# A GRU over 128 steps on one core: dummy products between the first sums, the candidate's first input products by groups, evictions between the splits of the recurrent weights, and a last step without splits

## What is computed

```python
def step(h, inp):
    x_t, prop = inp
    comb = jnp.concatenate([x_t, h], axis=-1)
    z = jax.nn.sigmoid(comb @ Wz + bz)
    r = jax.nn.sigmoid(comb @ Wr + br)
    comb2 = jnp.concatenate([x_t, r * h], axis=-1)
    h_cand = jnp.tanh(comb2 @ Wh + bh)
    h_new = (1.0 - z) * h + z * h_cand
    h_next = jnp.where(prop, jnp.tanh(h_new @ Wp + bp), h_new)
    return (h_next, h_new)
_, ys = jax.lax.scan(step, h0, (xs, do_prop))
```

## Time and profile before

| | |
|---|---|
| median of 3 runs | 1119.2 us |
| profiled execution | 1118.39 us |
| its span | 1116.6 us |
| PE busy | 1092.5 us |
| DVE busy | 672.9 us |
| ACT busy | 600.6 us |
| step 0's first recurrent matmul | 57.72 us after the span's start |

### The profile page before, as it was taken

How to read it: one execution, slowest core, us unless ns; L and a number is a source line. 1 busy time by engine, 2 the same in 40 slices (tenths; PEclk the granted TensorE clock), 3 DMA queues, 4 the chain that set the end, 5 groups by cost and what they waited for, 6 DMA issues and landing times.

```text
span 1116.6 us, 50158 instructions
## 1 busy us (share of the span) xinstructions
PE 1092.5 (98%) x22461; PEld 825.8 (74%) x22461; DVE 672.9 (60%) x2501; ACT 600.6 (54%) x1407; POOL 0.2 (0%) x4
## 2 busy tenths in 40 slices
PE   7799999999999999999999999999999999999996
PEld 3377777777777777777777777777777777779996
DVE  7876656655655655565565565556566555555656
ACT  4555545555554545555455464555555455455554
POOL 0000000000000000000000000000000000000000
PEclk8999999999999999999999999999999999999999
DMA  9001201002020020201102020020200201010001
GB/s 343 39 4 40 79 3 58 23 3 78 3 78 3 3 77 4 78 2 40 41 3 78 3 77 3 3 78 3 78 3 3 77 4 41 2 41 3 26 19 40
DMA packets 10294, 44.23 MB, mean 40 GB/s; under 512 B 1504, under 2 KB 2144, under 8 KB 6240
## 3 DMA queue, kind: packets, MB, share of 16 engines
q1 hardware_dynamic: 10080, 41.04, 9.8%
HBM read 24.26 MB, written 16.78 MB: 37 GB/s over the span
## 4 chain that ended last, share of the span: by engine, by line
PE 96%; DVE 2%; issue 1%; ACT 1%; DMA 0%; SPq 0%; DVEq 0%; ACTq 0%
PE acc L663 52%; PE x_acc L571 44%; DMA x_part<-wr_dram 0%; DVE wrec_lo L415 0%; DVE mag L359 0%; ACT gate L270 0%; DVE x_lo L422 0%; ACT x_hi L237 0%; DVE keep L514 0%; DVE h_split L528 0%; DVE new L519 0%; SPq L203 0%; DVE mag_win L434 0%; PE acc L577 0%; DVE mag_x L362 0%
## 5 line engine op out<-in xcount | busy, mean ns | idle before, releaser
L270 ACT ACTIVATE gate<-acc,unscale 128x128 f32<-128x128 f32 x702 | 239.5, 384 | 358.9 <-PE acc L663 356.4
L663 PE MATMUL acc<-h_split,wrec_hi 128*128 128x64 f16 x8192 | 343.8, 193 | 0.0
L571 PE MATMUL x_acc<-x_hi,win_hi 128*128 128x512 f16 (+1 forms) x816 | 300.7, 368 | 8.3 <-ACT x_part L251 5.6
L571 PE MATMUL x_acc<-x_hi,win_lo 128*128 128x512 f16 (+1 forms) x816 | 300.5, 368 | 0.0
L571 PE MATMUL x_acc<-x_lo,win_hi 128*128 128x512 f16 (+1 forms) x816 | 300.5, 368 | 0.0
L663 PEld LDWEIGHTS acc<-h_split,wrec_hi 128*128 128x128 f16 x8192 | 283.0, 98 | 0.0
L251 ACT ACTIVATE x_part<-x_acc,bias,part_unscale 128x512 f32<-128x512 f32 (+1 forms) x204 | 152.0, 751 | 130.6 <-PE x_acc L571 130.6
L663 PE MATMUL acc<-q_split,wrec_hi 128*128 128x64 f16 x5088 | 215.7, 193 | 0.4 <-issue 0.4
L663 PE MATMUL acc<-h_split,wrec_lo 128*128 128x64 f16 x4096 | 203.3, 193 | 4.2 <-DVE h_split L528 4.2
L663 PEld LDWEIGHTS acc<-h_split,wrec_lo 128*128 128x128 f16 x4096 | 163.2, 98 | 31.4 <-ACT acc L282 4.5
L663 PEld LDWEIGHTS acc<-q_split,wrec_hi 128*128 128x128 f16 x5088 | 179.2, 98 | 0.5 <-issue 0.5
(11 more groups left out here) (67 smaller groups left out, 633.7 us busy)
## 6 DMA issues: line engine op xcount, KB each, us to landing
x_blk<-x_dram SPq DMA_DIRECT2D x15, 1024.0 KB, 5.2
out_dram<-x_blk SPq DMA_DIRECT2D x15, 1024.0 KB, 3.9
x_blk<-x_dram SPq DMA_DIRECT2D x4, 256.0 KB, 4.2
x_part<-wr_dram SPq DMA_DIRECT2D x4, 256.0 KB, 5.6
x_part<-wz_dram SPq DMA_DIRECT2D x4, 256.0 KB, 5.8
x_part<-wh_dram SPq DMA_DIRECT2D x4, 256.0 KB, 6.2
x_part<-wr_dram SPq DMA_DIRECT2D x1, 1024.0 KB, 10.6
x_part<-wz_dram SPq DMA_DIRECT2D x1, 1024.0 KB, 12.8
```

Of the source, the lines that this page charges most:

```text
L270: nc.scalar.activation(gate[g][:, half, :], acc[g][:, half, :], func, scale=unscale[:, g:g + 1]).then_inc(gate_ready[g], 1)
L571: return nc.tensor.matmul(x_acc[bank][:, 0:cols], weights[g][:, k, j * P:(j + 1) * P], values[m % 2][:, k, steps.start * B:steps.stop * B] ...
L663: mm = nc.tensor.matmul(acc[g][:, j, :], weights[g][:, k, j * P:(j + 1) * P], values[:, k, lo, :], start=False, stop=False, skip_group_che ...
```

## The change

Five edits. (1) The 14 matmuls on constants become three bursts, of 8, 10 and 11 (`WARM`): before the sum of the input's magnitudes, between it and the sum of W_r's, and behind that. (2) DVE makes the input's scale after one of W_r's four magnitudes, not after two. (3) PE does the products of C by groups, and sums the magnitudes of block 1's input after Z's products, not after a quarter of C's; the sums for the recurrent weights stand inside C's groups; two groups of block 1 run before step 0 (`AHEAD`), not one; and each gate's recurrent weights are waited for where step 0 first uses them. (4) ACT evicts C's four groups and seeds R and Z between the three `split_rec`, not behind them. (5) At the last step DVE makes only the float32 state, without the hi and lo parts that no later step reads.

```diff
-WARM = 14
-AHEAD = 1
+WARM = (8, 10, 11)
+AHEAD = 2
...
-            for g in range(GATES):
-                split_rec(g)
-            for n in range(2 * KC, GROUPS):
+            split_rec(R)
+            for n in (2 * KC, 2 * KC + 1):
                 copy_group(n)
-            for g in range(GATES):
-                seed(g, 0)
+            split_rec(Z)
+            for n in (2 * KC + 2, 2 * KC + 3):
+                copy_group(n)
+            seed(R, 0)
+            seed(Z, 0)
+            split_rec(C)
+            seed(C, 0)
...
-                if k == 1:
+                if k == 0:
                     make_x_scale(0)
...
+                if t + 1 < T:
+                    for n, half in enumerate(HALVES):
+                        dve.wait_ge(new_ready, 2 * t + n + 1)
+                        nc.vector.tensor_tensor(split[:, half, 0, :], new[:, half, :], keep[:, half, :], ALU.subtract).then_inc(hi, 1)
                 for n, half in enumerate(HALVES):
                     dve.wait_ge(new_ready, 2 * t + n + 1)
-                    nc.vector.tensor_tensor(split[:, half, 0, :], new[:, half, :], keep[:, half, :], ALU.subtract).then_inc(hi, 1)
-                for half in HALVES:
                     nc.vector.tensor_tensor(h_out[:, half, :], new[:, half, :], keep[:, half, :], ALU.subtract).then_inc(h_new_ready, 1)
-                for n, half in enumerate(HALVES):
-                    dve.wait_ge(hi, count + n + 1)
-                    dve.wait_ge(h_new_ready, 2 * t + n + 1)
-                    subtract_hi(h_out, split, half).then_inc(lo, 1)
+                if t + 1 < T:
+                    for n, half in enumerate(HALVES):
+                        dve.wait_ge(hi, count + n + 1)
+                        dve.wait_ge(h_new_ready, 2 * t + n + 1)
+                        subtract_hi(h_out, split, half).then_inc(lo, 1)
+                else:
+                    dve.wait_ge(h_new_ready, 2 * t + 2)
...
+            def keep_going(count):
+                for n in range(count):
+                    nc.tensor.matmul(x_acc[BANKS - 1][:], ones[:], floor[:], start=True, stop=True)
...
-            for n in range(WARM):
-                nc.tensor.matmul(x_acc[BANKS - 1][:], ones[:], floor[:], start=True, stop=True)
+            keep_going(WARM[0])
             reduce_x_magnitude(0)
+            keep_going(WARM[1])
             pe.wait_ge(mag_ready[WIN + R], KC)
             for k in range(KC):
                 mm = add_magnitude(WIN + R, mag_win[:, k:k + 1])
             mm.then_inc(mag_reduced[WIN + R], 1)
-            for g in range(GATES):
+            keep_going(WARM[2])
+            for g in (R, Z):
...
-                    if (g, k) == (C, 0):
+                    if (g, k) == (Z, 3):
                         reduce_x_magnitude(1)
-                        reduce_magnitude(R)
-                    if (g, k) == (C, 1):
-                        reduce_magnitude(Z)
-                    if (g, k) == (C, 3):
-                        reduce_magnitude(C)
+            for k in range(KC):
+                pe.wait_ge(win_hi_ready[C], k + 1)
+                pe.wait_ge(win_lo_ready[C], k + 1)
+            fill(2 * KC * PER_GROUP, 2 * KC * PER_GROUP + PER_GROUP // 2)
+            reduce_magnitude(R)
+            fill(2 * KC * PER_GROUP + PER_GROUP // 2, (2 * KC + 2) * PER_GROUP)
+            reduce_magnitude(Z)
+            fill((2 * KC + 2) * PER_GROUP, (2 * KC + 3) * PER_GROUP + PER_GROUP // 2)
+            reduce_magnitude(C)
+            fill((2 * KC + 3) * PER_GROUP + PER_GROUP // 2, PER_BLOCK)
             fill(PER_BLOCK, PER_BLOCK + AHEAD * PER_GROUP)
```

More of the change, by code:

```diff
@@ L608, in fill @@
                     if c == 0:
-                        if n == GROUPS * m:
+                        if m and n == GROUPS * m:
                             pe.wait_ge(x_hi_ready, KC * (m + 1))
@@ L667, in _ @@
             LOW, HIGH = range(KC)[HALVES[0]], range(KC)[HALVES[1]]
-            for g in range(GATES):
-                pe.wait_ge(wrec_hi_ready[g], 1)
-                pe.wait_ge(wrec_lo_ready[g], 1)
             for t in range(T):
@@ L674, in _ @@
                 first, middle, last = fill_of(t)
+                if t == 0:
+                    pe.wait_ge(wrec_hi_ready[R], 1)
+                    pe.wait_ge(wrec_lo_ready[R], 1)
                 pe.wait_ge(seed_ready[R], t + 1)
@@ L684, in _ @@
                 rec(R, wrec_hi, h_split, LOW, 1)
+                if t == 0:
+                    pe.wait_ge(wrec_hi_ready[Z], 1)
+                    pe.wait_ge(wrec_lo_ready[Z], 1)
                 pe.wait_ge(seed_ready[Z], t + 1)
@@ L694, in _ @@
                 rec(Z, wrec_hi, h_split, HIGH[:1], 1)
+                if t == 0:
+                    pe.wait_ge(wrec_hi_ready[C], 1)
+                    pe.wait_ge(wrec_lo_ready[C], 1)
                 pe.wait_ge(seed_ready[C], t + 1)
```

## The result

The changed kernel takes 1109.01 us (median of 6 runs, 1108.75 to 1110.24) against 1118.88 for the one before (6 runs, 1118.54 to 1119.97): 9.9 us less, ratio 0.9912 with a 95% interval of 0.9900 to 0.9925. The prediction said 1108.6 and faster. The profiled execution has a span of 1106.8 us, where 1105.8 was worked out.

The account below looks back on a forecast made before the run. PE, busy 98% of the span, was taken as the bound, with losses before step 0. Terms -7.8 - 2.6 + 0.2 + 0.1 - 0.7 = -10.8 from 1118.39 gave 1107.6, forecast as 1108.6, range 1107.2 to 1111.6 us.

Parts of the forecast that it names:

- The ledger of 10.2 us: PE's loss before step 0: 2.5 clock at start, 5.6 pause, 1.2 clock after it, some 0.9 short waits and sums.
- PE's start: Before the first product: with three bursts it comes at 13.45 us, where it was 13.73.
- The clock: Before step 0: stays full with no PE pause over 1.6 us; otherwise at half for 5.07 us.
- DVE 5.45 us ahead: DVE before step 0: goes on at 34.5 us after the sum for block 1's input, 5.45 us ahead.
- margin: Time by which each operand or bank PE needs before or in step 0 comes early; three are 1.0 to 1.2 us.
- ACT's order: Before block 1's first group: eviction done at 40.4 us against 44.7 needed; behind all three splits it made the 5.63 us pause.
- Step 0: Start of the steps: at 49.95 us instead of 57.72, -7.8 us, with one group more done.
- The steps of block 0: 120 products to fill instead of 132: -2.6 us, with +0.2 and +0.1 coming back as waits.
- The last step: End of the kernel: x_blk starts at 1112.73 instead of 1113.39, -0.66 us.
- the first: Rival, chance 0.17: first burst too short, clock rises late or falls, or bursts don't hold it; 1110.1 to 1112.4 us.
- The second: Rival, chance 0.08: DVE is not as far ahead, idle time becomes waits elsewhere on DVE; 1112.8 us, half of it 1110.
- the third: Rival, chance 0.03: no better or slower, clock stays at half while products run; 1142 us were all 168 slow.

Follow-up runs that it names:

- run 1: The changed kernel with all constants matmuls in one burst of 14 before the first sum, none between the sums: 1110.0 us, ratio 0.9918.
- run 10: The changed kernel with bursts of 8, 3 and 3 instead of 8, 10 and 11: 1109.34 us, ratio 0.9915.
- run 4: The changed kernel with one group of block 1 before step 0 instead of two: 1110.12 us, ratio 0.9921.
- run 5: The changed kernel with the sum of block 1's input magnitudes behind 108 products instead of 96: 1110.93 us, ratio 0.9934.
- run 3: The changed kernel with ACT's old order, three splits, then C's four evictions, then the seeds: 1114.06 us, ratio 0.9956.
- run 12: The changed kernel with block 0's store, and block 4's load behind it, issued four steps later: 1108.3 us, ratio 0.9904.
- run 9: The changed kernel with a first burst of 14 matmuls instead of 8: 1108.46 us, ratio 0.9906.
- run 11: The changed kernel with bursts of 8, 3 and 3 and block 1 products moved from later steps to step 2 onward: 1109.17 us, ratio 0.9913.
- run 6: The changed kernel with the hi and lo parts made at the last step too, as before: 1109.35 us, ratio 0.9917.
- run 7: The changed kernel with products of block 1 moved earlier, four from steps 4 to 7 to step 2: 1108.53 us, ratio 0.9908.
- run 2: The kernel before with the three bursts of 8, 10 and 11 and nothing else of the change: 1117.24 us, ratio 0.9986.

## Why the prediction was right, and where it was off

- **The ledger of 10.2 us** was right in kind and nearly in size. PE's start: 13.22 for 13.45. Half of the difference is a transfer that landed 0.1 us earlier (W_r's first quarter: DVE's first mag_win at 7.81, in the earlier trace rows at 7.93).
- **The clock** held with bursts of 8, 10 and 11, and without them it falls (run 1). The 2.5 us that I gave it were this trace's 12 slow products; in run 1 they were six, 1.3 us. The reason that I gave, no pause over 1.6 us, does not hold: the longest was 1.82 us and the clock stayed, while run 10 lost it with no pause over 1.80. The clock was forecast rightly, for a wrong reason and so partly by luck. What differed is that the changed kernel does ten and eleven matmuls between the pauses, and run 10 three and three; how many are needed between three and ten was not tried.
- **DVE 5.45 us ahead** at the sum for block 1's input: it is 39.95 - 34.30 = 5.65. The first state's hi part, forecast for 48.7, ends at 48.16 + 0.36 = 48.5. No margin was reached, and runs 4 and 5 show that they were as thin as written.
- **ACT's order** was the 5.63 us: run 3 brings the pause back, at 3.46 us for the 3.5 expected.
- **Step 0**: 49.73 for 49.95; lead 7.99 for 7.8. **The steps of block 0**: 10.24 - 7.99 = 2.25 for 2.3, with the 0.89 us before step 3's C part as forecast. **The last step**: 0.66 to 0.69 for 0.66.
- **The term that was missing**: "From block 1 on every step has the same work." It has, but not the same waits. PE waits 1.1 us in the changed kernel and 0.4 before for its own instructions (cause shown for step 8, by run 12 and its packets), and the lead falls by 1.1 us in all between steps 8 and 127. That is the whole difference between the span worked out (1105.8) and measured (1106.8). Nor is it so that between the steps nothing can be won but by fewer or faster matmuls: run 12 won 0.4 us there by moving a store.
- **The rivals**: the first has two mechanisms. A clock that rises late came in the changed kernel itself, in its second profile (eight matmuls in 3.62 us, in the first in 2.53), and cost nothing; with a longer burst it cost 0.4 us (run 9). A clock that falls came in runs 10 and 11, with shorter bursts, and in neither profile of the changed kernel. The prediction had no run to show how far the start varies; these two profiles do. One of its six runs is 1.0 to 1.5 us above the others (1110.24). Its mean granted clock is 0.998, the others' 0.999 to 1.000, which points to the clock, but there is no trace of it. The second and the third did not come.

The wait at step 120 has the same mark, though no run moved its transfer. In the changed kernel a store runs from 1049.64 to 1052.68 us. After the one at 1044.63 no packet of PE's instructions starts until 1052.67, and PE stands until 1054.87, 2.2 us after that. In run 9, with twelve instructions more ahead, the packet starts at 1050.10, before the store, and there is no wait. In all fourteen profiles an issue wait at step 8 or 120 ends 2.2 to 2.5 us after the start of a packet that comes within 0.3 us of a store's end, and always at the same count of PE's instructions (3,521 and 42,945, give or take one). So more or fewer instructions ahead put another matmul of the step at that count. The length varies too: at step 120 0.77 us with 29 constants matmuls, but 0.49 and 1.04 in runs 6 and 7, which change DVE's order or the fill, and 1.04 in run 2; 0.33 to 0.39 with 14; none with 35.

Open: the wait at step 127 (0.15 us, none in the second profile, 0.42 in run 12). The store nearest to it starts after its packet of instructions.

## What to carry to other kernels

Before a long loop that one engine fills, write down each chain that leads to its first step and compare them by their margins: here four edits that look unrelated (a sum 12 products earlier, evictions between splits, a second group ahead, dummy products) each took away the wait that would have come next. Undoing one of the first three cost 1.1 to 5 us, and undoing the bursts 1.0; these are medians, and only the 5 has an interval clear of the changed kernel's. Dummy matmuls that keep the clock were ten and eleven here, in the 2.5 to 2.8 us before each sum's or product's operand came, where three and three lost it; and they must not run over the moment at which the real operand comes, also when the clock rises late. A gain of a microsecond in an early stage can be taken back by waits for instructions a thousand microseconds later; look for idle time that names no other engine inside runs of equal instructions, compare leads at several steps, not only ends, and see whether a packet of the engine's instructions starts late there, at the end of a large transfer.

## What was not expected of the hardware

- PE stands for 0.15 to 1.04 us within a run of like matmuls at places that are fixed for a program and move with the number of instructions ahead: at step 8, 0.19 and 0.26 us in two profiles of the changed kernel, 0.56 with six more matmuls, none with fifteen fewer, and none when a 1 MB store and the 1 MB load behind it are moved away. At steps 8 and 120 each such wait ends 2.2 to 2.5 us after the start of a 16 KB packet of instructions that came only at the end of a 1 MB store.
- The eight matmuls of the first burst took 2.53 us in one profile of the changed kernel and 3.62 in the other: when the clock rises differs by more than 1 us between executions of one kernel.
- The granted clock fell after bursts of three matmuls (0.8 us) with pauses of 1.1 and 1.8 us around them, near 9.9 us, and in another profile between 8 and 9; with ten in that place it stayed whole. Back at full it came 2.7, 3.5, 5.1 and 5.3 us after the first product in four profiles (runs 1 and 10, the kernel before, and run 11).
